# Feed-forward stages: h is divided by its scales on GpSimd between two VectorE steps that overlap over pairs of tiles, and the down products stand behind the next gate and up products

## The reference, cut to what matters

```
def fp4_quant_dequant(x):            # blocks of 16 along the last dimension
    scale = maximum(max(abs(xb)) / 6.0, 1e-12)
    xn = xb / scale
    q = GRID[searchsorted(MID, abs(xn))] * sign(xn) * scale   # GRID 0, 0.5, 1, 1.5, 2, 3, 4, 6
def fp4_linear(x, w): return einsum('bsk,nk->bsn', fp4_quant_dequant(x), fp4_quant_dequant(w))
gate = fp4_linear(x, w_gate)         # 128 -> 352
y    = fp4_linear(x, w_up)           # 128 -> 352
h    = silu(gate) * y
out  = fp4_linear(h, w_down)         # 352 -> 128
```

## Time and profile before

| | |
|---|---|
| median of 3 runs | 928.35 us (927.18 to 928.64) |
| profiled execution | 928.58 us |
| its span | 926.8 us |
| TensorE busy | 753.7 us (81%) |
| VectorE busy | 673.2 us (73%) |
| ScalarE busy | 371.1 us (40%) |
| GpSimd busy | 390.2 us (42%) |
| mean granted clock of TensorE | 0.923 of 2.4 GHz |

### The profile page before, as it was taken

One profiled execution on the slowest core, in us unless ns is written; L12 is line 12 of the kernel. 1 busy time (PEld: TensorE's weight loads), 2 busy tenths in 40 slices (PEclk: granted clock), 3 DMA queues, 4 the chain that ended last, 5 costly groups with the idle time before them and its releaser, 6 DMA issues. The chain is left out here.

```text
span 926.8 us, 16478 instructions
## 1 busy us (share of the span) xinstructions
PE 753.7 (81%) x6055; PEld 497.7 (54%) x6055; DVE 673.2 (73%) x1165; ACT 371.1 (40%) x646; POOL 390.2 (42%) x559
## 2 busy tenths in 40 slices
PE   0578888899989997768874977599999998985693
PEld 0356457788878986346543644244444443553462
DVE  7889777999977799899651338789999995363132
ACT  3113760111116611223411524078888888341151
POOL 3444014888773140355254535223333333126353
PEclk9989898999999999899896989589999999979697
DMA  3000000000000000500112123574000000011113
GB/s 84 0 1 1 1 1 1 1 1 1 1 1 2 1 1 1 171 1 1 40 38 34 39 74 108 164 127 77 10 9 10 10 10 10 7 46 41 28 41 114
DMA packets 33396, 30.28 MB, mean 33 GB/s; under 512 B 6598, under 2 KB 27654, under 8 KB 33318
## 3 DMA queue, kind: packets, MB, share of 16 engines
q1 hardware_dynamic: 29678, 22.37, 9.6%
q0 software_dynamic: 2944, 6.04, 2.7%
q10 hardware_dynamic: 696, 0.82, 0.4%
HBM read 16.89 MB, written 10.35 MB: 29 GB/s over the span
## 5 line engine op out<-in xcount | busy, mean ns | idle before, releaser
L2246 DVE TENSOR_REDUCE blockmax<-c_bank 128x8 f32<-128x1024 f32 x144 | 173.1, 1220 | 21.0 <-PE c_bank L2377 16.6
L2307 ACT ACTIVATE PT<-c_bank 128x1024 f32<-128x1024 f32 x144 | 146.9, 1027 | 36.7 <-PE c_bank L2399 34.4
L2413 PE MATMUL c_bank<-PT,V 128*9 128x256 f32 (+1 forms) x1408 | 87.0, 344 | 3.7 <-ACT OT L2299 2.6
L2370 PE MATMUL c_bank<-KA,QA 48*128 48x128 bf16 (+3 forms) x608 | 60.6, 284 | 23.9 <-DMA KA<-PT 8.8
L2196 POOL TENSOR_SCALAR_AFFINE_SELECT PT<-PT 128x256 f32<-128x256 f32 x128 | 49.1, 407 | 69.8 <-ACT PT L2307 69.8
L1007 PE MATMUL sums<-prod,ident 128*128 128x128 f32 x512 | 67.4, 288 | 9.5 <-DVE prod L1080 8.7
L1007 PEld LDWEIGHTS sums<-prod,ident 128*128 128x128 f32 x512 | 62.0, 198 | 17.0 <-DVE prod L1080 13.4
L1556 POOL DMA_INDIRECT routed_results<-results_m,target_m x46 | 44.5, 968 | 52.3 <-DVE results_m L1812 49.5
L400 PE MATMUL gu_f<-gu_wT,xqT_f 128*128 128x352 f32 x128 | 49.5, 533 | 13.9 <-DVE h_f L320 11.1
L2399 PE MATMUL c_bank<-QA,KA 51*128 51x128 bf16 (+3 forms) x480 | 57.1, 301 | 0.7 <-DVE blockmax L2246 0.7
L1835 DVE TENSOR_TENSOR r_h_m<-r_silu_m,m_bank_m 128x256 f32<-128x256 f32 x46 | 19.3, 421 | 52.2 <-ACT r_silu_m L1735 52.2
(11 more groups left out here) (379 smaller groups left out, 1773.4 us busy)
## 6 DMA issues: line engine op xcount, KB each, us to landing
scaled_rows<-xs_m SPq DMA_DIRECT2D x8, 256.0 KB, 2.2
back_m<-routed_results SPq DMA_DIRECT2D x8, 256.0 KB, 3.7
qk_parts_dram<-PT SPq DMA_DIRECT2D x8, 256.0 KB, 2.7
qk_parts_dram<-PT SPq DMA_DIRECT2D x4, 384.0 KB, 3.5
QA<-qk_parts_dram SPq DMA_DIRECT2D x6, 256.0 KB, 4.5
KA<-qk_parts_dram SPq DMA_DIRECT2D x6, 256.0 KB, 6.5
m_gu<-in_rt_gate SPq DMA_DIRECT2D x1, 1024.0 KB, 5.8
m_gu<-in_rt_up SPq DMA_DIRECT2D x1, 1024.0 KB, 8.3
```

The source lines that it names most:

```text
L2246: nc.vector.tensor_reduce(blockmax[:, h % 2, :, HALFQ * n:HALFQ * (n + 1)], slot_of((1, m)).rearrange("p b (n c) -> p b n c", c=P), AX.X, ...
L2307: nc.scalar.activation(PT[:, u % PRING, :, :], slot_of((0, u)), ACT.Exp, scale=SCALE).then_inc(s_pt, 1)
L2370: ins = nc.tensor.matmul(out[:, b, n * P:end * P], QA[at, h, PLACE[i] * P:(PLACE[i] + 1) * P], KA[at, h, spot * P:(spot + end - n) * P], s ...
L2413: ins = nc.tensor.matmul(O[32 * g:32 * g + DH + 1, f * P:f * P + n], V[:, b, j, h, :], PT[:, u % PRING, b, o:o + n], start=(a % len(VALUES ...
```

## The change

Division of h by its scales moves from VectorE to GpSimd. `Quant.on_vector` is cut in three: `inverse` (maximum, scale, reciprocal), `divide`, and `lifted` (AND, constant, sum). For x all three still run on VectorE. For h, VectorE makes h(j + 1) and its reciprocals (`inverse_h(j + 1)`) and then lifts h(j) (`lifted_h(j)`); GpSimd divides h(j + 1) ahead of rounding and scaling h(j). `h`, `xs` and `inv` get two buffers, `scale` three. Block maxima and reciprocals lie in SBUF and no longer in PSUM, and with that TensorE's wait within gate_up is gone. x group 3 goes ahead of the pairs, behind `inverse_h(0)`. TensorE's loop becomes gate_up(j + 2), project(j - 1), turn_h(j), residual(j); ScalarE's silu(j + 2), residual(j - 1), hidden columns(j). The last pair still ends in halves.

```diff
-    def __init__(self, k, tag, width, ctx, spare=None):
+    def __init__(self, k, tag, width, ctx, ahead=1):
-        small = spare if spare is not None else k.sb(f"q_small{tag}", [P, 2 * self.nb], ctx=ctx)[:, :]
-        self.amax, self.inv = small[:, 0:self.nb], small[:, self.nb:2 * self.nb]
-        self.scale = k.sb(f"q_scale{tag}", [P, 2, self.nb], ctx=ctx)
-        self.xs = k.sb(f"q_xs{tag}", [P, width], ctx=ctx)
+        self.amax = k.sb(f"q_amax{tag}", [P, self.nb], ctx=ctx)
+        self.inv = k.sb(f"q_inv{tag}", [P, ahead, self.nb], ctx=ctx)
+        self.scale = k.sb(f"q_scale{tag}", [P, 3, self.nb], ctx=ctx)
+        self.xs = k.sb(f"q_xs{tag}", [P, ahead, width], ctx=ctx)
...
+    def inverse(self, ch, src, n, at=0):
+
+        nc = self.nc
+        ch.link(nc.vector.tensor_reduce(self.amax[:, :], self.blocks(src), AX.X, ALU.max, apply_absolute_value=True))
+        ch.link(nc.vector.tensor_scalar(self.scale[:, n % 3, :], self.amax[:, :], 1.0 / 6.0, 1e-12, ALU.mult, ALU.max))
+        return nc.vector.reciprocal(self.inv[:, at, :], self.scale[:, n % 3, :])
+
+    def divide(self, eng, src, at=0):
+        return eng.tensor_tensor(self.blocks(self.xs[:, at, :]), self.blocks(src), self.spread(self.inv[:, at, :]), ALU.mult)
+
+    def lifted(self, ch, n, s_y, halves=False, at=0):
+
+        nc, xs, magic, y = self.nc, self.xs[:, at, :], self.magic[:, n % 2, :], self.y[:, n % 2, :]
         ch.link(nc.vector.tensor_scalar(magic.bitcast(I32), xs.bitcast(I32), EXPONENT_BITS, None, ALU.bitwise_and))
         ch.link(nc.vector.tensor_scalar(magic, magic, 1.0, GRID_MAGIC, ALU.max, ALU.mult))
+            nc.vector.scalar_tensor_tensor(y, xs, ONE_BELOW, magic, ALU.mult, ALU.add).then_inc(s_y, 1)
             return
...
+    def on_vector(self, ch, src, n, s_y):
+
+        ch.link(self.inverse(ch, src, n))
+        ch.link(self.divide(self.nc.vector, src))
+        self.lifted(ch, n, s_y)
...
+    def on_gpsimd_scale(self, dst, n):
+        return self.nc.gpsimd.tensor_tensor(self.blocks(dst), self.blocks(self.y[:, n % 2, :]),
+                                            self.spread(self.scale[:, n % 3, :]), ALU.mult)
...
-        h = k.sb(f"h{tag}", [P, 2, FF], ctx=ctx)
+        h = k.sb(f"h{tag}", [P, 2, 2, FF], ctx=ctx)
-        qx = Quant(k, f"x{tag}", XTILES * D, ctx, y[:, 1, 2 * D:2 * D + 2 * XTILES * D // QBLOCK])
-        qh = Quant(k, f"h{tag}", W2, ctx, gu[:, 1, 1, FF:FF + 2 * W2 // QBLOCK])
+        qx = Quant(k, f"x{tag}", XTILES * D, ctx)
+        qh = Quant(k, f"h{tag}", W2, ctx, ahead=2)
+        pair = lambda j: h[:, j % 2].rearrange("p s c -> p (s c)")
...
+                def inverse_h(j):
                     dve.wait_ge(s_silu, j + 1)
-                    nc.vector.tensor_tensor(h[:, :, :], silu[:, :, :], gu[:, :, 1, 0:FF], ALU.mult).then_inc(s_h, 1)
+                    nc.vector.tensor_tensor(h[:, j % 2], silu[:, :, :], gu[:, :, 1, 0:FF], ALU.mult).then_inc(s_h, 1)
                     dve.wait_ge(s_h, j + 1)
+                    wait(dve, s_hq, j - 2)
+                    qh.inverse(chh, pair(j), j, j % 2).then_inc(s_hinv, 1)
+
+                def lifted_h(j):
+                    dve.wait_ge(s_hxs, j + 1)
                     wait(dve, s_hq, j - 1)
-                    qh.on_vector(chh, h[:, :, :].rearrange("p s c -> p (s c)"), j % 2, s_hy, j == LAST)
+                    qh.lifted(chh, j, s_hy, j == LAST, j % 2)
...
                 for g in range(XG - 1):
                     quantise_x(g)
+                inverse_h(0)
+                quantise_x(XG - 1)
                 for j in range(PAIRS):
-                    quantise_h(j)
-                    if j in XAFTER:
-                        quantise_x(XAFTER[j])
+                    if j + 1 < PAIRS:
+                        inverse_h(j + 1)
+                    lifted_h(j)
...
+                def divide_h(j):
+                    pool.wait_ge(s_hinv, j + 1)
+                    wait(pool, s_hy, j - 1)
+                    qh.divide(nc.gpsimd, pair(j), j % 2).then_inc(s_hxs, 1)
...
                 for g in range(XG - 1):
                     finish_x(g)
+                divide_h(0)
+                finish_x(XG - 1)
                 for j in range(LAST):
+                    divide_h(j + 1)
                     finish_h(j)
-                    if j in XAFTER:
-                        finish_x(XAFTER[j])
...
-                            if j >= 1 and s == m == 1:
-                                pe.wait_ge(s_hdve, Quant.LINKS * (j - 1) + Quant.SCALED)
                             ins = nc.tensor.matmul(gu[:, s, m, 0:FF], xt, k.gu_wT[:, m * FF:(m + 1) * FF], start=True, stop=True)
                     ins.then_inc(s_gu, 1)
                     pe.wait_ge(s_hq, j + 1)
-                    pe.wait_ge(s_xqT, XG if j > 1 else XG - 1)
+                    pe.wait_ge(s_xqT, XG)
...
                 def residual(j):
                     wait(pe, s_res, j - 1)
-                    if j == 1:
-                        pe.wait_ge(s_xdve, Quant.LINKS * (XG - 1) + Quant.SCALED)
...
                 for j in range(PAIRS):
                     if j + 2 < PAIRS:
...
+                    if j == 0:
+                        turn_x(XG - 1)
+                    else:
+                        project(j - 1)
...
                     turn_h(j)
-                    if j in XAFTER:
-                        turn_x(XAFTER[j], j + 1)
                     residual(j)
-                    project(j)
...
                 for j in range(LAST):
                     if j + 2 < PAIRS:
                         gate(j + 2)
+                    if j == 0:
+                        columns(XG - 1)
+                    else:
+                        residual(j - 1)
                     hidden_columns(j)
-                    if j in XAFTER:
-                        columns(XAFTER[j])
-                    if j >= 1:
-                        residual(j - 1)
```

More of the change, by code:

```diff
@@ L187, in on_vector @@
[L187 to L194, removed]
@@ L196, in scale_half @@
-    def scale_half(self, eng, dst, slot, s):
-        by = self.scale[:, slot, s * self.nb // 2:(s + 1) * self.nb // 2].unsqueeze(2).to_broadcast([P, self.nb // 2, QBLOCK])
-        return eng.tensor_tensor(self.blocks(dst), self.blocks(self.y[:, slot, self.half(s)]), by, ALU.mult)
+        one, two = (self.half(s) for s in range(2))
+        nc.vector.scalar_tensor_tensor(y[:, one], xs[:, one], ONE_BELOW, magic[:, one], ALU.mult, ALU.add).then_inc(s_y, 1)
+        ch.link(nc.vector.scalar_tensor_tensor(y[:, two], xs[:, two], ONE_BELOW, magic[:, two], ALU.mult, ALU.add))
@@ new lines, in lifted, with on_gpsimd_round @@
+        ch.link(nc.vector.tensor_tensor(y[:, two], y[:, two], magic[:, two], ALU.subtract))
+    def on_vector(self, ch, src, n, s_y):
+        ch.link(self.inverse(ch, src, n))
+        ch.link(self.divide(self.nc.vector, src))
+        self.lifted(ch, n, s_y)
+    def on_gpsimd_round(self, n, at=slice(None)):
+        return self.nc.gpsimd.tensor_tensor(self.y[:, n % 2, at], self.y[:, n % 2, at], self.magic[:, n % 2, at], ALU.subtract)
+    def on_gpsimd_scale(self, dst, n):
+        return self.nc.gpsimd.tensor_tensor(self.blocks(dst), self.blocks(self.y[:, n % 2, :]),
+                                            self.spread(self.scale[:, n % 3, :]), ALU.mult)
@@ L201, with scale_half @@
+    def scale_half(self, eng, dst, n, s):
+        by = self.scale[:, n % 3, s * self.nb // 2:(s + 1) * self.nb // 2].unsqueeze(2).to_broadcast([P, self.nb // 2, QBLOCK])
+        return eng.tensor_tensor(self.blocks(dst), self.blocks(self.y[:, n % 2, self.half(s)]), by, ALU.mult)
 class Prepare:
@@ L276, in fp4_ffn @@
     XTILES = TILES // XG
-    XAFTER = {1: 3}
     with ExitStack() as ctx:
@@ L371, in _, with turn_x @@
                     finish_x(g)
+                divide_h(0)
+                finish_x(XG - 1)
                 for j in range(LAST):
+                    divide_h(j + 1)
                     finish_h(j)
-                    if j in XAFTER:
-                        finish_x(XAFTER[j])
                 pool.wait_ge(s_hy, PAIRS)
-                qh.on_gpsimd_round(LAST % 2, qh.half(0)).then_inc(s_hround, 1)
+                qh.on_gpsimd_round(LAST, qh.half(0)).then_inc(s_hround, 1)
                 pool.wait_ge(s_hround, PAIRS)
                 pool.wait_ge(s_tp, LAST)
-                qh.scale_half(nc.gpsimd, hq[:, 0, :], LAST % 2, 0).then_inc(s_hq, 1)
+                qh.scale_half(nc.gpsimd, hq[:, 0, :], LAST, 0).then_inc(s_hq, 1)
             @block.tensor
             def _(pe):
-                def turn_x(g, evicted):
+                def turn_x(g):
                     pe.wait_ge(s_xq, g + 1)
-                    wait(pe, s_hqT, evicted)
                     wait(pe, s_xqT, g - 1)
@@ L449, in _ @@
                     keep_busy(k, y[:, 0, :], 9)
-                turn_x(0, 0)
+                turn_x(0)
                 if prepare:
@@ L454, in _ @@
                 gate_up(0)
-                turn_x(1, 0)
```

(3 more changed lines are left out.)

23 lines of the change are left out of this document (8 added, 15 removed).

## The result

The changed kernel takes 956.05 us (median of 4 runs, 952.14 to 960.76); the kernel before, on the same chip, 927.76 us (4 runs, 926.55 to 928.64). The ratio on record is 1.0318, with a 95% interval of 1.0291 to 1.0344: slower, as forecast, but by 28.3 us and not by 17.4, and above the range.

What follows compares the result with a forecast made beforehand. VectorE set the 5.58 us pair; after the change, VectorE and GpSimd steps in a row at their shared port give 6.85. Each of two stages gains 8.7 us: 928.58 + 17.4 = 946 us, range 932 to 955.

Steps and rivals of the forecast that it cites:

- steps 1 to 3: Settled pairs: division leaves VectorE (minus 0.92), costs GpSimd 1.39, and shared-port steps stand in a row: 6.85 us a pair.
- step (5): Stage head: in x groups 1 and 2 scale step and division wait for GpSimd, +0.75 each; head 32.8 us.
- step (4): TensorE's order: gate_up(j + 3) behind turn_h(j) makes h(j + 3) 0.96 late, harmless up to S + 1.35 (S: sum's end); two-pair loop 12.25.
- clock rival: TensorE's gap of about 1.7 us in each pair lowers its clock to 1.2 GHz: +12, 958; chance 0.09.
- the forecast's own sum of the second stage: Second feed-forward stage: head 32.8, five pairs 34.3, last pair 4.1, tail 6.2: 77.4 against 68.7, +8.7.
- Project behind gate_up costs nothing: TensorE's loop: the moved down products run in its idle time ahead of turn_h, at no cost.
- Only the loop of 6.1: Lower bound: only TensorE's two-pair loop sets pairs, 12.25 / 2 = 6.1 us, 2.7 + 2 of head a stage: 938.
- the bound with a free scale step: Settled pairs: if VectorE's scale step never waits for GpSimd, 6.23 us a pair, 0.6 less: 939.
- From a lower granted clock: First feed-forward stage: the reason given for its being 2.39 us longer before; it was given the same +8.7.
- faster: Rival: the port is not the limit and hq comes early enough, pairs fall to 4.7: -10.6, 918; chance 0.09.
- nothing: Rival: port mostly free, TensorE's loop at 6.1 a pair, gains elsewhere give it back: 925 to 931; chance 0.05.
- half of it: Rival: VectorE wins the race for the gap between GpSimd's round and scaling: 931 to 938; chance 0.09.

Runs made afterwards that it cites:

- Kernel 7: Changed kernel with gate_up(j + 3) at the loop heads, GpSimd dividing only 16 of 704 columns (result incomplete): 924.69 us, ratio 0.9986.
- kernels 4: Changed kernel with division of h back on VectorE and gate_up(j + 3), silu(j + 3) at the loop heads: 935.77 us, ratio 1.0108.
- kernel 5: Changed kernel, h divided on VectorE behind its reciprocal, gate_up(j + 3) and silu(j + 3) first, block maxima and reciprocals in PSUM: 927.79 us, ratio 0.9995.
- Kernel 1: Changed kernel with three idle 512-column TensorE matmuls ahead of turn_h of pairs 0, 2, 4 and 6: 945.98 us, ratio 1.0222.
- 11: Changed kernel with three idle TensorE matmuls ahead of turn_h of pairs 1, 3 and 5: 947.23 us, ratio 1.0235.
- kernel 8: Kernel before with only the down products of pair j - 1 behind gate_up(j + 2), residual copy ahead of hidden columns: 926.43 us, ratio 1.0017.
- kernel 2: Changed kernel with gate_up(j + 3) and silu(j + 3), not j + 2, at the loop heads: 937.93 us, ratio 1.0123.
- kernel 9: Changed kernel, gate_up(j + 3) and silu(j + 3) at loop heads, block maxima and reciprocals of x in PSUM, of h in SBUF: 934.70 us, ratio 1.0132.

## Why the prediction was right, and where it was wrong

The direction and most of the mechanism held; the size was short by 10 us (956.09 against 946).

- *The port (steps 1 to 3)* was right. AND, division and constant came in the forecast order, the constant at 1.58 to 1.59 ("about 1.6"), the division at 1.54 to 1.67 where it waited. The scale step and division of x groups 1 and 2 came too, as step (5) has them:

```profile
391.11 0.75 DVE L173 TENSOR_SCALAR q_scalex_f<-q_amaxx_f 128x32 f32<-128x32 f32 x1
...
392.29 1.23 DVE L177 TENSOR_TENSOR q_xsx_f<-xn_f,q_invx_f 128x512 f32<-128x512 f32 x1
```

  (0.18 and 0.69 in x group 0, beside an idle GpSimd.) Kernel 7 shows the cause by its price. The Trainium skill's rule (SBUF — State Buffer, "SBUF: two separate sides") of a lock held for a whole instruction agrees with kernels 4 and 5: the same division takes 1.65 with its inverse in SBUF and 0.89 with it in PSUM, beside the same scaling.
- *That the pairs come evenly at 6.85 us* was wrong in a way that mattered. Two pairs were to take 13.7 us; they took 14.56, 15.81 and 14.74, as one slow and one fast pair. In the fast one, 6.15, the scale step found the 0.08 us gap between GpSimd's two steps, which the forecast had it miss. Kernel 1, with the same order and no low clock, came back to nearly even pairs.
- *The step that failed is (4), with the clock rival that rests on it:* h(j + 3) "0.96 behind the next pair's sum", taken for every pair, and with it the rival's gap of "about 1.7 in each pair". VectorE's wait for silu is 0 in one pair and up to 4.2 us in the next, TensorE's gap 0 in one pair and 3.4 to 5.3 us in the next. Step (4) had "turn and residual 1.11, gate and up 2.57" at the high clock in every pair; in the slow pairs turn, residual and gate and up together took 1.4 to 2.7 longer. The trace of before had the row that prices such a gap, 3.56 us and then 4.24 for gate and up, and the forecast weighed only gaps of 1.7 against it. It had a fall behind shorter gaps too, which the forecast overlooked: 2.55 us, a turn of 0.66, 0.68 us, and then

```profile
384.50 4.14 PE L400 MATMUL gu_f<-gu_wT,xqT_f 128*128 128x352 f32 x8 [0.68 <-ACT xqT_f L481]
```

  The two-pair loop in step (4) was a hint, as far as one can argue: turn_h(j) releases h(j + 3), and nothing in it makes two neighbours alike. The rival's price, 958, came close to the 956 measured, though its way there (1.7 of lateness in every pair) did not happen; its chance of 0.09 was far too small. One of the forecast's own signs of being wrong, gate and up at 4 us in a settled pair, did show (4.10). Whether the low clock made the pairs uneven or only kept them so isn't separated: kernel 1 filled the gaps and kept the clock at once.
- *The missed term, by the forecast's own sum of the second stage:* head 32.61 (forecast 32.8), five pairs 38.96 (34.3), last pair 3.97 (4.1), tail 9.08 (6.2). What is over in the pairs and the tail are the chains behind turns at the low clock. Turn to project took 4.88, 6.12 and 5.06 us for 3.45, that is 1.43, 2.67 and 1.61 more, 5.7 in all. VectorE's waits for silu in the same pairs were 2.99, 4.23 and 3.17: without the excess, 1.56 each time. So at the high clock the slow pair would be 6.98, and five pairs 33.25: 1.05 under the forecast, which hid a part of the miss. In the tail turn_h(6) took 1.54, its residual 1.06 and the down products 2.11 for 1.50; from turn_h(6) to the last turn it was 5.84 us, 3.34 in kernel 1. The first stage came to 84.69 for 79.8. Kernel 1 took this term away and came to 945.98. That idle matmuls work by the clock and by nothing else isn't shown by a clean control (11); clock, durations and time moved together in both.
- *"Project behind gate_up costs nothing"*: right within 0.4%, as far as kernel 8 shows it, which is the kernel before with this move and not the changed one.
- *"Only the loop of 6.1"* as a lower bound was never reached, as port and loop held each other; freed of the loop, the pair is 6.15 (2), where the bound with a free scale step said 6.23. The loop of 12.25 was too short in itself: it has 1.95 for the lift, but behind a late h the constant still waits for the division (424.84 to 427.84 is 3.00), and with it two pairs come to some 13.2. And the bound worked out from it doesn't add up: 2.7 and 2 in each of two stages are 9.4, which gives 937 and not 938.
- *"From a lower granted clock"*, said of the 2.39 us by which the first stage was longer before: the earlier trace rows has 0.95 for both. The trace shows it in VectorE's waits for silu, 4.88 us in the first stage and 2.45 in the second, and in the gate and up of the earlier trace rows, which took 5.03 in the first stage.
- *The other rivals:* faster, nothing and half of it are out. For 4.7 us a pair the port would have to be free (7: 5.09 with nearly no division, as AND still stands behind the scaling).

What stays open: why kernel 5 gained only 1.25 us ahead of the tail in the first stage (in the second the gain was there and the tail took it back), and why the clock in the tail is low in one stage or kernel and not in another. Whether the inverse's move to SBUF cost the changed kernel anything while the loop bound it wasn't measured.

## What to carry to other kernels

Before moving a step to the engine that shares a port, add up the port time of both, not each engine's busy time: here the division was 0.89 us on VectorE, where it met nobody, and a GpSimd step of 1.39 us behind which VectorE's constant stood. When an edit puts the producer of a later pair behind the consumer of an earlier one, follow the loop over as many pairs as it spans and let them be unequal; then ask of the longest gap, not of the mean one, what the clock does. Where a small operand lies can decide whether a long step waits, so an operand's move is priced at every step that reads it.

## What the runs showed of the hardware

- A waiting engine needs very little to get in: in x group 1 the 32-column scale step stood behind GpSimd's round (to 391.82) and was over at 391.86, ahead of the scaling that started at 391.91. In the pairs 0.08 us between two GpSimd steps let the 44-column step through at 0.19 us, and the scaling behind it took its usual 1.39.
- The small step waits as a large one does: with its input in SBUF the 32-column scale step took 0.75 us behind GpSimd; the 44-column one took 0.20 from PSUM within GpSimd's scaling.
- GpSimd's product with a spread 44-column operand takes 1.39 us for 704 columns, and the same on 16 columns 0.50.
- Behind the gaps of 3.4 to 5.3 us in the settled pairs of the changed kernel TensorE ran at 1.2 GHz (granted 0.50 to 0.59 in the stretches shown); behind gaps of 0.9 to 1.3 us, as in kernel 1, gate and up took 2.53 us each time. In between, the length of the gap alone doesn't settle it: behind the same 3.02 us the turn of pair 6 took 1.54 us in kernel 2 and 0.88 in kernel 9, and behind 2.03 us it took 1.29 in the second stage of kernel 5 and 0.88 in the first.
